# A causal mask moved from TensorE to VectorE: identity matmuls against an add in the accumulator

## The reference, cut to what matters

```python
scores = jnp.einsum('bqhd,bkhd->bhqk', q, k)
scores = scores + jnp.einsum('bqr,bkr->bqk', q_rope, k_rope)[:, None]
scores = scores / scale
causal = jnp.triu(jnp.ones((Tt, Tt), dtype=bool), k=1)
scores = jnp.where(causal[None, None], -jnp.inf, scores)
w = jax.nn.softmax(scores, axis=-1)
attn = jnp.einsum('bhqk,bkhd->bqhd', w, v).reshape(Bb, Tt, D_MODEL)
```

## Time and profile before

| | |
|---|---|
| median of 3 runs | 3565.42 us (3564.26 to 3568.84) |
| profiled execution | 3564.22 us, its span 3562.3 us |
| instructions | 49452 |
| TensorE busy | 2294.1 us (64%) |
| VectorE busy | 1926.6 us (54%) |
| ScalarE busy | 1229.1 us (35%) |

### The profile page before, as it was taken

The page is one execution under the profiler, slowest core; times in us unless marked ns, Lnnn a source line. Parts: engine busy times, 40 slices in busy tenths (PEclk is TensorE's granted clock), DMA queues, the critical chain, the costliest instruction groups (busy, mean ns, idle before and its releaser), DMA issues. The chain is left out here.

```text
span 3562.3 us, 49452 instructions
## 1 busy us (share of the span) xinstructions
PE 2294.1 (64%) x13288; PEld 1203.0 (34%) x13288; DVE 1926.6 (54%) x5734; ACT 1229.1 (35%) x2019; POOL 317.0 (9%) x349
## 2 busy tenths in 40 slices
PE   3479999997652177679999999963222629413180
PEld 1124343433431155224343444342221516312060
DVE  4566666663358863656565566637730146775012
ACT  3324554554342244624344444413211313312040
POOL 0100000000000000000000000000024250002516
PEclk9769999999775588779999999986655959765595
DMA  3353435430100000521112121130002440000145
GB/s 113 95 105 59 96 78 94 79 59 14 39 3 1 0 7 7 159 63 51 50 49 57 44 58 43 40 115 1 1 19 75 127 42 0 2 1 10 60 143 71
DMA packets 149123, 189.64 MB, mean 53 GB/s; under 512 B 26817, under 2 KB 92097, under 8 KB 148801
## 3 DMA queue, kind: packets, MB, share of 16 engines
q1 hardware_dynamic: 137632, 159.69, 18.3%
q0 software_dynamic: 11264, 27.28, 4.2%
HBM read 126.73 MB, written 60.16 MB: 52 GB/s over the span
## 5 line engine op out<-in xcount | busy, mean ns | idle before, releaser
L678 ACT ACTIVATE at_probs<-at_score 128x1024 f32<-128x1024 f32 (+7 forms) x1024 | 653.5, 650 | 875.0 <-PE at_score L603 540.4
L703 DVE CUSTOM_DVE_ANT_0 at_masked<-at_mx,g_maskw 128x512 bf16<-128x512 f32 (+3 forms) x1024 | 482.8, 485 | 182.8 <-PE at_mx L569 176.2
L569 PE MATMUL at_mx<-at_K,at_Q 96*128 96x512 bf16 (+7 forms) x1536 | 466.5, 344 | 117.8 <-DVE at_mpart L703 40.4
L601 PE MATMUL at_score<-at_Q,at_K 96*128 96x512 bf16 (+7 forms) x1536 | 504.3, 332 | 28.9 <-issue 14.3
L603 PE MATMUL at_score<-at_Q,at_K 98*128 98x512 bf16 (+7 forms) x1536 | 507.0, 331 | 0.0
L699 DVE TENSOR_REDUCE at_mpart<-at_mx 128x1 f32<-128x512 f32 x512 | 353.3, 690 | 264.0 <-PE at_mx L569 245.2
L623 PE MATMUL at_outp<-at_probs,at_vop 128*32 128x512 f32 (+6 forms) x3072 | 445.3, 497 | 0.0
L569 PEld LDWEIGHTS at_mx<-at_K,at_Q 120*128 120x128 bf16 (+1 forms) x1536 | 148.3, 98 | 438.2 <-DVE at_mpart L703 198.6
L601 PEld LDWEIGHTS at_score<-at_Q,at_K 120*128 120x128 bf16 (+1 forms) x1536 | 149.8, 98 | 339.4 <-issue 183.3
L606 PE MATMUL at_score<-g_maskkq,g_identb 128*128 128x128 bf16 x1024 | 225.5, 221 | 0.0
L623 PEld LDWEIGHTS at_outp<-at_probs,at_vop 128*32 128x32 f32 (+1 forms) x3072 | 125.2, 122 | 108.2 <-issue 61.8
(11 more groups left out here) (455 smaller groups left out, 3466.5 us busy)
## 6 DMA issues: line engine op xcount, KB each, us to landing
at_Q<-q SPq DMA_DIRECT2D x192, 128.0 KB, 2.9
at_Q<-qr SPq DMA_DIRECT2D x72, 256.0 KB, 7.1
at_K<-kr SPq DMA_DIRECT2D x72, 256.0 KB, 8.7
q<-p_pieces SPq DMA_DIRECT2D x40, 384.0 KB, 3.3
at_K<-k SPq DMA_DIRECT2D x168, 64.0 KB, 2.2
o<-at_osb SPq DMA_DIRECT2D x64, 128.0 KB
n_oc<-o SPq DMA_DIRECT2D x8, 1024.0 KB, 5.2
at_Q<-q SPq DMA_DIRECT2D x96, 64.0 KB
```

Source lines behind the costliest of these rows:

```text
L569: pe.matmul(bank[:, 0:hi - lo], Q0[0:R, g % 4, j, qt * P:(qt + 1) * P], K0[0:R, g % 4, j % KG, lo:hi], start=True, stop=True).then_inc(s_m ...
L601: pe.matmul(bank, K0[0:R0, g % 4, j % KG, kb * P:(kb + 1) * P], Q0[0:R0, g % 4, j, lo:hi], start=True, stop=False)
L678: act.activation(probs[:, kb % 2, j, kb * P:T], src, ACT.Exp, scale=cf.scale).then_inc(s_exp, 1)
L703: dve.tensor_tensor_reduce(masked[:, u % 2, 0:w], mx[:, u % 2, 0:w], k.maskw[:, CH - w:CH], 1.0, NEG, ALU.add, ALU.max, mpart[:, part, j, ...
```

## The change

The mask of the score blocks that feed the exponentials is added by VectorE. The third matmul goes; `mask_diagonal` reads the diagonal block of 128 by 128 from the score buffer, adds `maskkq` and writes it back in place. The exponential waits for a new semaphore `s_dg` that this operation raises, no longer for `s_st`. Since VectorE must now follow the scores, its maxima are no longer one run of units but are interleaved: a mask, then the units of the same head and key block, in TensorE's order. `finish_max` and `copy_turned` move behind the masks of key block 4.

```diff
@@ scores
-                    diag = lo == kb * P
                     bank = score[:, u % 2, half, lo - half * CH:CH]
...
                     last = pe.matmul(bank, K1[0:R1, g % 2, j % KG, kb * P:(kb + 1) * P], Q1[0:R1, g % 2, j, lo:hi],
-                                     start=False, stop=not diag)
-                    if diag:
-                        last = pe.matmul(bank[:, 0:P], k.identb[:], k.maskkq[:], start=False, stop=True)
+                                     start=False, stop=True)
                 last.then_inc(s_st, 1)
@@ step on ScalarE
-                        act.wait_ge(s_st, n * U + u + 1)
+                        act.wait_ge(s_dg, n * U + u + 1)
@@ VectorE
+            def mask_diagonal(b, g, kb, j):
+                u = kb * G + j
+                block_ = score[:, u % 2, kb // 4, kb % 4 * P:(kb % 4 + 1) * P]
+                dve.wait_ge(s_st, (b * GN + g) * U + u + 1)
+                dve.tensor_tensor(block_, block_, k.maskkq[:], ALU.add).then_inc(s_dg, 1)
@@ step on VectorE
-                    wide_maxima(*one)
-                if two:
-                    reduce_units(*two, NARROW, 0)
+                u1, u2 = NARROW_U, 0
+                for kb in range(QT):
+                    for j in range(G):
+                        mask_diagonal(b, g, kb, j)
+                        if kb in WIDE and one:
+                            u1 = reduce_unit(*one, j, WIDE[kb], u1)
+                        if kb in NARROW and two:
+                            u2 = reduce_unit(*two, j, NARROW[kb], u2)
+                    if kb == 4 and one:
+                        finish_max(*one, u1)
+                        copy_turned(*one, u1)
```

More of the change, by code:

```diff
@@ L428, in attention @@
         s_st, s_exp, s_pv = c.sem("scores_ready"), c.sem("probs_ready"), c.sem("values_done")
-        s_dpassed = c.sem("vector_passed")
+        s_dpassed, s_dg = c.sem("vector_passed"), c.sem("diagonal_masked")
         s_mx, s_mxf = c.sem("max_scores_ready"), c.sem("max_scores_read")
@@ L688, in _, with reduce_unit @@
             dve.sem_inc(s_os[1], 16 * (G + 1))
+            def reduce_unit(b, g, j, qts, u):
+                n = b * GN + g
+                for qt in qts:
+                    for part in range(2 if qt >= 4 else 1):
+                        w = min((qt + 1) * P, (part + 1) * CH) - part * CH
+                        dve.wait_ge(s_mx, n * MU + u + 1)
+                        if part * CH + w < (qt + 1) * P:
+                            dve.reduce_max(mpart[:, part, j, qt:qt + 1], mx[:, u % 2, 0:w],
+                                           AX).then_inc(s_mxf, 1)
+                        else:
+                            dve.sem_inc(s_dpassed, 1)
+                            dve.tensor_tensor_reduce(
+                                masked[:, u % 2, 0:w], mx[:, u % 2, 0:w], k.maskw[:, CH - w:CH], 1.0, NEG, ALU.add,
+                                ALU.max, mpart[:, part, j, qt:qt + 1]).then_inc(s_mxf, 1)
+                        u += 1
+                return u
@@ L690, in reduce_units @@
             def reduce_units(b, g, parts, u):
-                n = b * GN + g
                 for qts in parts.values():
                     for j in range(G):
[L694 to L706, removed]
@@ L707, in reduce_units @@
-                return u
+                        u = reduce_unit(b, g, j, qts, u)
+                return u
+            def mask_diagonal(b, g, kb, j):
[3 more added lines that the diff above has]
+                dve.tensor_tensor(block_, block_, k.maskkq[:], ALU.add).then_inc(s_dg, 1)
             def finish_max(b, g, u):
```

## The result

The changed kernel takes 3658.55 us (median; 3652.74 to 3661.62), the kernel before, in the runs beside it, 3566.3 us. The ratio is 1.0256, with a 95% interval of 1.0239 to 1.0274: the change makes the kernel 2.6% slower. The profiled execution took 3661.62 us; its span is 97.4 us longer than before's.

The account below looks back on a forecast made before the run. The prediction saw TensorE as the bound only on the surface, held in key blocks 0 to 3 in a loop with VectorE over `mx`'s two banks. Terms 16 + 54 + 10 + 4 + 18 = +102 us gave 3668 us, range 3610 to 3755.

Parts of the forecast that it names:

- Key block 4: `finish_max` behind the masks delays TensorE's transposes: 1.35 us a step in at0, 1.1 in at1, 54 us in all.
- Key block 7: Masks lengthen the bare chain of tiny units: 0.45 us a step in at1, 0.25 in at0, 18 us in all.
- Start of a step: The first mask stands ahead of VectorE's first maximum: +0.20 us in each of 48 steps, 10 us.
- Key block 5: The mask lengthens VectorE's queue: last max matmul 0.25 us later in at0, 4 us in all; at1 0.
- Key blocks 0 to 3: VectorE's queue sets the pace with the masks in it: 0.13 us a head, 8 us in each attention, 16 us slower.
- for 512 columns I take 0.70: Key blocks 0 to 3: time in VectorE's queue from a masked maximum of 512 columns to the next operation, 0.70 us.
- The mask's own length: VectorE's mask of 128x128 lasts 0.28 us, takes 0.20 us of the queue, starts 0.08 us after its scores.
- The clock: Rival: stalls drop TensorE to 1.2 GHz for a quarter of the windows' work, +283 us, 3950 us; chance 4%.
- So TensorE can win at most 61 us: Removing 1024 mask matmuls, each with a 0.06 us issue gap, saves TensorE at most 61 us, 1.7% of the time.
- The faster rival: Masks vanish in VectorE's idle third and TensorE keeps its 61 us, less 10 at the starts: 3515 us; chance 4%.
- The hidden chain: Rival: the delay at the transposes is absorbed later in the step, without the 54 us: 3614 us; chance 7%.
- VectorE as the pace of every unit: Rival: each of 1024 masks takes 0.20 us of the loop, 205 us, with 54 + 14 more: 3840 us; chance 7%.

Follow-up runs that it names:

- e1: The changed kernel with `finish_max` moved ahead of the masks of key block 4, masks still on VectorE: 3590.35 us, 1.0074 against the kernel before.
- e3: The kernel before, mask matmuls kept, with `finish_max` made to wait for the last scores of key block 4: 3624.86 us, 1.0166 against the kernel before.
- e4: The kernel before without the mask matmuls, nothing masked, exponential scale a hundredth: 3543.46 us, 0.9934 against the kernel before.
- e7: The changed kernel with the mask matmuls put back, so the mask is added twice: 3680.47 us, 1.0322 against the kernel before.
- e9: The changed kernel with the mask behind the maxima of its head in key blocks 0 to 3: 3762.88 us, 1.0549 against the kernel before.
- e6: As e5, with the mask on VectorE in key block 6 too: 3559.17 us, 0.9984 against the kernel before.
- e5: e1 with the mask on VectorE only in key blocks 1, 2 and 3, mask matmuls elsewhere: 3556.02 us, 0.9970 against the kernel before.
- e2: The changed kernel with each mask on one column instead of 128, exponential scale a hundredth: 3627.39 us, 1.0174 against the kernel before.
- e8: The changed kernel again, nothing edited, for a second profile: one execution, 3662.51 us.

## Why the prediction was right

The forecast was 3668 us, 3610 to 3755 and slower; 3658.55 us was measured. Its largest steps held, one had the wrong sign, and two costs were missed or put too low. That the sum comes within 10 us is in part luck: key blocks 0 to 3 were put some 23 us too high, and about as much was left out, some 10 us for the clock, 4 to 5 outside the attentions, 6 in key block 7 and 3 in key block 4.

- **Key block 4 (54 us): right, and shown.** The piece to the transposes grew by 1.40 us in the table's step of at0 and 1.48 in the earlier ones (1.35 put), and by 1.12 in at1 (1.1 put): 56 to 57 us. e1 takes it away and wins 65 to 68 us, e3 has it alone and loses 59. The trace after puts the same names on it: VectorE waits for scores, then TensorE for `finish_max`.
- **Key block 7 (18 us): right in at1, too low in at0.** +0.45 in at1, as put. In at0 it is +0.34 in the table's step but +0.59 in those of the first three batches (0.25 put): 23 us in all. That "more work of TensorE lies beside it" did not help there: the block has four units in two buffers, and the third one's scores wait 0.47 us for the first one's exponential (the row at 315.29 above). The rows below, of at1's key block 7 in the timeline of the changed kernel, show the chain that was forecast: the second exponential ends at 1995.59, 1.40 us behind the first score matmul, where I had 1.49 and the earlier trace rows have 0.90.

```profile
1994.19 0.23 PE L600 MATMUL at_score<-at_Q,at_K 96*128 96x128 bf16 x1
...
1994.52 0.30 DVE L714 TENSOR_TENSOR at_score<-at_score,g_maskkq 128x128 f32<-128x128 f32 x1 [0.24 <-PE at_score L602]
...
1994.98 0.29 DVE L714 TENSOR_TENSOR at_score<-at_score,g_maskkq 128x128 f32<-128x128 f32 x1
...
1995.31 0.28 ACT L675 ACTIVATE at_probs<-at_score 128x128 f32<-128x128 f32 x1 [0.18 <-DVE at_score L714]
```

- **Start of a step (10 us): right in size.** +0.20 in at1's key block 0, +0.14 in at0's.
- **Key block 5 (4 us):** +0.39 in at0 (0.25 put), but -0.12 in at1 (0 put): 6 - 4 = 2 us.
- **Key blocks 0 to 3 (16 us): the sign was wrong.** Beyond the start of the step nothing was lost: key blocks 2 and 3 gained 0.11 us in at0 and 0.13 in at1, and key block 1 kept its length within 0.07. The step that failed is "for 512 columns I take 0.70". The mask follows the masked maximum after 0.61 us (811.55 to 812.16 in the rows below), and the 0.66 of the earlier trace rows held a short wait for the max matmul, which the timeline didn't label: that matmul ended only at about 1903.20, and the maximum started at 1903.24. So VectorE needs 0.20 + 0.60 + 0.61 = 1.41 us a head, below the 1.50 of key block 0. In key block 1 my step gives 1.28 us with this number, again no more than now. That the mask matmul "gives nothing back here" was wrong too: VectorE's queue is not the limit, and the matmul that is gone gives the 0.11 and 0.13 us, as e4 shows.
- **The mask's own length:** 297 ns against 280; it takes 0.20 to 0.21 us of the queue, as put. It starts 0.04 us behind its scores (0.08 put).
- **The clock: missed as a small cost.** The rival put it at a quarter of the work and +283 us. What came is 56 us at the lower level instead of 13, and about 10 us by the steps; the profiled pair of e7 agrees with 8 to 11. The Trainium skill ("TensorE: Matmul & The Clock Gate", section "A second HAM failure mode: psum-queue depth-cycling") tells of a kernel where small idle gaps made the clock swing. The trace of the change shows such a swing in at0, 0.95 in its window; but e3, with the same gap in every step, has 14 us of it, and e4, with no gap added, has 45, so the gaps alone don't decide it.
- **"So TensorE can win at most 61 us":** a correct bound, but far from what is there. e4 measures 23.
- **The faster rival** is refuted at the point I named: nothing stands between the last score and the transposes. The section of the Trainium skill named with it ("Perfetto Trace Analysis", "Identifying the Most-Contended Engine") was read too shortly: it does not take the busy share of matmuls for TensorE but the arithmetic done and the busy share of weight loads. By weight loads TensorE has 230 of 568 us in the earlier trace rows, below VectorE's 379, so the section doesn't clearly point to TensorE here. **The hidden chain** is refuted too: the pieces after the transposes don't give the 1.1 us back. **VectorE as the pace of every unit** needed that masks wait and nothing runs beside them; e9 comes to more than half of its 275 us with the same instructions in another order.

The rows in which the failed step shows, at0's key block 0 in the changed kernel:

```profile
810.75 0.29 DVE L714 TENSOR_TENSOR at_score<-at_score,g_maskkq 128x128 f32<-128x128 f32 x1
810.96 0.68 DVE L694 TENSOR_REDUCE at_mpart<-at_mx 128x1 f32<-128x512 f32 x1
811.55 0.68 DVE L698 CUSTOM_DVE_ANT_0 at_masked<-at_mx,g_maskw 128x512 bf16<-128x512 f32 x1
...
812.16 0.29 DVE L714 TENSOR_TENSOR at_score<-at_score,g_maskkq 128x128 f32<-128x128 f32 x1
```

Each operation starts some 0.08 us before the end of the one ahead: 810.75 + 0.29 = 811.04, and the next starts at 810.96. By the rule that the prediction took from the Trainium skill ("VectorE: DVE Perf Modes", section "The DRAIN you can't avoid") the mask would hold the queue for its whole length, and it doesn't. The same section adds that an operation which is not held starts earlier, which the prediction left out and these rows agree with.

What stays open is why TensorE's clock falls in some steps of at0 and which ones. Fewer mask matmuls (the change, e4, e9, e6 against e5) go with more of it, and e7 gives it back, but e1 and e2 have as few of them and only 9 and 24 us of it. Only the change was profiled twice, so small differences such as that of e5 and e6 may be chance. No run settled it.

## What to carry to other kernels

When an operation moves to another engine, list what its new wait holds up in that engine's queue before asking how long the operation lasts: here four operations of 0.17 us, held for 1.1 us in front of an engine that waited for them, made 60% to 75% of the loss, and a mask of one column still cost two thirds of it. An operation ahead of one that had to wait anyway was free here, and the same operation one place later cost 104 us. A removed matmul was worth its whole issue gap only where TensorE was not held by a loop; leave it out altogether once, as e4 does, to see about how much a move can win. And read more than one step: the one of at0 in the table shows little more than half of what key block 7 costs in most others.

## What the runs showed of the hardware

- The in-place tensor_tensor of 128x128 float32 on the accumulator lasts 297 ns on VectorE and holds its queue for 0.20 to 0.21 us.
- The matmul behind a mask matmul starts 0.06 us after it, 61 us for 1024, but taking all out wins 23 us (e4), and adding them to the change costs 22 to 24 (e7).
- TensorE, idle for 1.15 us, goes on 0.13 us behind the end of the operation on VectorE that it waits for (e3), and 0.14 in the change (1987.46 + 0.17 to 1987.77); I had put 0.05.
- TensorE's granted clock drops to 0.50 (1.2 GHz) for stretches of 3.4 to 13.7 us (the change, e8) in a stage where the engine is busy 88% of the time (547.88 of 620 us). In the two profiled executions the amount is alike (56 and 57 us), the places aren't. A microsecond at the lower level cost this stage about a quarter of one (an estimate from five steps).
